# Cross attention of one layer: the queries put into the four row groups by sixteen on-chip transfers, and the order of TensorE, ScalarE and GpSimd that goes with it

## What is computed

```python
w1, w2, w3 = (w_sim[:d], w_sim[d:2 * d], w_sim[2 * d:])
Sim = (encoder_hc @ w1)[:, :, None] + (decoder_hq @ w2)[:, None, :] + jnp.einsum('bid,bjd->bij', encoder_hc * w3, decoder_hq) + b_sim[0]
A = jax.nn.softmax(Sim, axis=2)
hq_hat = jnp.einsum('bij,bjd->bid', A, decoder_hq)
Batt = jax.nn.softmax(jnp.max(Sim, axis=2), axis=1)
hc_bar = jnp.einsum('bi,bid->bd', Batt, encoder_hc)[:, None, :]
hc_hat = jnp.broadcast_to(hc_bar, encoder_hc.shape)
feats = jnp.concatenate([encoder_hc, hq_hat, encoder_hc * hq_hat, encoder_hc * hc_hat], axis=-1)
hcq = feats @ W_qv + b_qv
```

## Time and profile before

| | |
|---|---|
| median of 3 timed runs | 1349.12 us (1347.23 to 1350.66) |
| the profiled execution | 1346.48 us, of which span 1344.7 us |
| busy, PE | 1229.2 us (91%), x10417 |
| busy, DVE / POOL / ACT | 733.2 us (55%) / 708.3 us (53%) / 337.5 us (25%) |
| attention, from the span's start to the last store of x1 | about 690 us |
| the rest (recurrence, experts) | about 655 us, not touched |

### The profile page before, as it was taken

The page is one execution under the profiler, slowest core; times in us unless marked ns, Lnnn a source line. Parts: engine busy times, 40 slices in busy tenths (PEclk is TensorE's granted clock), DMA queues, the critical chain, the costliest instruction groups (busy, mean ns, idle before and its releaser), DMA issues. The chain is left out here.

```text
span 1344.7 us, 29581 instructions
## 1 busy us (share of the span) xinstructions
PE 1229.2 (91%) x10417; PEld 732.7 (54%) x10418; DVE 733.2 (55%) x1573; ACT 337.5 (25%) x768; POOL 708.3 (53%) x762
## 2 busy tenths in 40 slices
PE   0899999999999999999979799999499999999994
PEld 0444434444434444434447556666388888888883
DVE  4555666555566555567249768888722322332335
ACT  2222233222233232233135311112311111111110
POOL 1055534355544355544229766787297653540872
PEclk9999999999999999999979899999599999999997
DMA  8645554435564445554145568863214444321556
GB/s 284 227 147 205 212 211 134 155 143 200 211 211 138 151 146 197 211 211 143 70 153 163 156 214 274 293 212 111 101 48 150 146 156 149 127 83 62 149 167 185
DMA packets 99376, 225.45 MB, mean 168 GB/s; under 512 B 14152, under 2 KB 30664, under 8 KB 95216
## 3 DMA queue, kind: packets, MB, share of 16 engines
q1 hardware_dynamic: 87872, 189.46, 41.0%
q0 software_dynamic: 10288, 33.57, 7.4%
q10 hardware_dynamic: 1152, 1.57, 0.4%
HBM read 179.21 MB, written 45.35 MB: 167 GB/s over the span
## 5 line engine op out<-in xcount | busy, mean ns | idle before, releaser
L326 POOL TENSOR_TENSOR wb<-w,hcb 128x512 f32<-128x512 f32 x120 | 122.3, 1040 | 314.7 <-DVE hcb L683 292.6
L401 PE MATMUL S<-ctxT,x 32*64 32x416 f32 (+1 forms) x4096 | 185.1, 511 | 15.9 <-DVE ctxT L627 15.9
L401 PEld LDWEIGHTS S<-ctxT,x 32*64 32x64 f32 x4096 | 108.7, 133 | 94.5 <-issue 45.8
L329 POOL TENSOR_TENSOR wb<-wb,w 128x512 f32<-128x512 f32 x120 | 150.2, 1273 | 0.0
L609 DVE STREAM_TRANSPOSE ctxT<-ctx_one 128x1024 f32<-128x1024 f32 (+1 forms) x128 | 115.0, 949 | 11.7 <-DMA ctx_one<-in_ctx_dram 11.5
L436 PE MATMUL O<-ctx_one,probsT 128*64 128x512 f32 (+1 forms) x448 | 110.4, 608 | 0.0
L522 ACT ACTIVATE x<-S,w2R,w3R 128x128 f32<-128x128 f32 x256 | 92.9, 474 | 19.5 <-PE S L392 19.5
L1938 POOL TENSOR_TENSOR w_low<-w_low,w_high 128x2048 fp32r<-128x2048 f32 x21 | 96.8, 4611 | 1.7
L2123 DVE TENSOR_TENSOR f_hL<-f_TH,f_hH 128x512 fp32r<-128x512 f32 x39 | 27.0, 693 | 120.4 <-ACT f_hH L2076 117.3
L634 DVE TENSOR_REDUCE mx<-S 128x1 f32<-128x832 f32 x16 | 16.4, 1025 | 128.1 <-PE S L401 128.1
L1454 PE MATMUL Pb<-WrT,yT 128*32 128x128 f32 x2016 | 69.0, 278 | 8.3 <-DVE yT L1714 7.7
(11 more groups left out here) (286 smaller groups left out, 2504.8 us busy)
## 6 DMA issues: line engine op xcount, KB each, us to landing
ctx_one<-in_ctx_dram SPq DMA_DIRECT2D x64, 512.0 KB, 4.5
x<-in_ctx_dram SPq DMA_DIRECT2D x16, 1536.0 KB
ctx_two<-in_ctx_dram SPq DMA_DIRECT2D x16, 1536.0 KB, 9.3
ctx_one<-in_ctx_dram SPq DMA_DIRECT2D x64, 256.0 KB, 5.5
w_low<-_L_ffn_gate_up_proj_dram POOLq DMA_DIRECT2D x10, 1024.0 KB, 8.0
f_xt<-routed_x SPq DMA_DIRECT2D x39, 256.0 KB
routed_y<-f_yt SPq DMA_DIRECT2D x39, 256.0 KB
w_low<-_L_ffn_gate_up_proj_dram SPq DMA_DIRECT2D x6, 1024.0 KB, 8.6
```

The costliest lines, as they stand in the source:

```text
L326: pool.tensor_tensor(wb[:, slot, b], w3[:, c], hcb[:, c, b, None].to_broadcast([P, D]), ALU.mult).then_inc(wb_step, 1)
L329: pool.tensor_tensor(wb[:, slot, b], wb[:, slot, b], w0[:, c], ALU.add).then_inc(wb_ready, 1)
L401: last = pe.matmul(S[64 * b:64 * b + 64, a, 0:tiles * Q], qr[a * Q:(a + 1) * Q, k, 64 * b:64 * b + 64], ctxT[a * Q:(a + 1) * Q, 0:tiles, b ...
```

## The change

PE no longer spreads. `turn_early(f)` transposes the normed tokens into O (free at that time) directly behind the scores of the pair before; ACT's `queries(f)` takes it with w3c and w2c (now one column for each chunk of 128 features) into the new tile q3; and `replicate` issues sixteen transfers of 32 partitions x 512 elements from q3 into qr, on SP ahead of everything else in its step (for the first pair on ACT's queue). The scores wait for q_in, which counts them. `turn_tokens` and hcT remain for the own product.

The own product of chunk 0 stands behind the values, that of chunk 1 behind the turning of hqh, and Y's accumulation begins with it. The multiplication in the own weights goes from POOL to ACT (`scale_own`); POOL keeps the addition. brow's product goes from n=5 to n=3 of the values, and DVE's look-ahead transpose 5 goes behind hcb.

```diff
-        qr = x2[:, 2 * TWO:2 * TWO + C, :].rearrange("p c (e i) -> p (c e) i", e=QUADS)
+        qr = x2[:, 2 * TWO:2 * TWO + C, :].rearrange("p e (c i) -> p e c i", c=C)
+        q3 = sb("q3", [P, C, P])
...
+        def replicate(eng):
+            for e in range(QUADS):
+                for a in range(QUADS):
+                    eng.dma_start(qr[a * Q:(a + 1) * Q, e], q3[e * Q:(e + 1) * Q]).then_inc(q_in, 16)
...
-                for a in range(QUADS):
-                    rows = slice(a * Q, (a + 1) * Q)
-                    sp.dma_start(w2R[rows, :], w_sim[D:2 * D].rearrange("(k s) -> s k", s=Q)).then_inc(const_in, 16)
-                    sp.dma_start(w3R[rows, :], w_sim[2 * D:3 * D].rearrange("(k s) -> s k", s=Q)).then_inc(const_in, 16)
+                sp.dma_start(w2c[:], w_sim[D:2 * D].rearrange("(c p) -> p c", p=P)).then_inc(const_in, 16)
+                sp.dma_start(w3c[:], w_sim[2 * D:3 * D].rearrange("(c p) -> p c", p=P)).then_inc(const_in, 16)
...
+                sp.wait_ge(q_ready, C * (p + 2))
+                replicate(sp)
...
             def own_weights(p, c):
 
                 slot = c % 2
-                if later(p, 1) or c >= 2:
-                    pool.wait_ge(wb_used, C * p + c - 1)
-                for b in range(2):
-                    pool.tensor_tensor(wb[:, slot, b], w3[:, c], hcb[:, c, b, None].to_broadcast([P, D]), ALU.mult).then_inc(wb_step, 1)
...
-                    pool.wait_ge(hcb_done, p + 1)
...
+            def turn_early(f):
+
+                pe.wait_ge(hc_ready, f + 1)
+                for c in range(C):
+                    last = pe.transpose(O[:, c * P:(c + 1) * P], tok_rows[:, c * P:(c + 1) * P], ident[:])
+                last.then_inc(q_full, 1)
...
                 pe.wait_ge(hqh_ready, p)
+                pe.wait_ge(q_ready, C * (p + 1 if step == "last" else p + 2))
...
-                    if n == 2 and step != "last":
-                        spread_queries(p + 1, 1 - s, (0, 1))
...
-                    if n == 5:
+                    if n == 3:
...
                     values(p, s, step)
-                    if front:
-                        spread_queries(f, fs, (2, 3))
+                    pe.wait_ge(hcb_step, p + 1)
+                    own_product(p, s, (0,))
                     pe.wait_ge(hqh_ready, p + 1)
                     turn_tile(0, "hqh", tok_rows, p, step)
+                    own_product(p, s, (1,))
...
-                    product(hqT, 0, range(C), True)
-                    own_product(p, s, range(half))
+                    product(hqT, 0, range(C))
...
-                    pe.wait_ge(q_ready, DB * (f + 1))
+                    pe.wait_ge(q_in, 16 * QUADS * QUADS * (f + 1))
+                    pe.wait_ge(hcT_ready, f + 1)
                     scores().then_inc(qk_done, 1)
+                    if loads is not None:
+                        turn_early(f + 1)
...
+            def scale_own(p, c):
+
+                if later(p, 1) or c >= 2:
+                    act.wait_ge(wb_used, C * p + c - 1)
+                for b in range(2):
+                    act.activation(wb[:, c % 2, b], w3[:, c], ACT.Copy, scale=hcb[:, c, b:b + 1]).then_inc(wb_step, 1)
+
...
+                    act.activation(q3[:, c, :], O[:, c * P:(c + 1) * P], ACT.Identity,
+                                   scale=w3c[:, c:c + 1], bias=w2c[:, c:c + 1]).then_inc(q_ready, 1)
...
+                if step == "full":
+
+                    act.wait_ge(hcb_done, p + 1)
+                    if first(p):
+                        act.wait_ge(wqv_in, 32)
+                    scale_own(p, 0)
+                    scale_own(p, 1)
...
-                if front:
-                    queries(f, 2)
-                    queries(f, 3)
+                if step == "full":
+                    scale_own(p, 2)
+                    scale_own(p, 3)
                 if loads is not None:
 
                     act.wait_ge(s1_ready, f + 1)
                     norm(f + 1)
+                    queries(f + 1)
...
-                    turn_ahead(f, fs, None, (4, 5))
+                    turn_ahead(f, fs, None, (4,))
...
+                if front and back:
+                    turn_ahead(f, fs, None, (5,))
```

More of the change, by code:

```diff
@@ L123, in cross_attention @@
         bqv_b = sb("bqv_b", [P, D])
-        spread = sb("spread", [P, P])
-        w2R = sb("w2R", [P, DB])
-        w3R = sb("w3R", [P, DB])
+        w2c, w3c = sb("w2c", [P, C]), sb("w3c", [P, C])
         bsim_b = sb("bsim_b", [P, 1])
@@ L172, in cross_attention @@
         xb_ready = sem("xb_ready")
-        q_full, q_ready = sem("q_full"), sem("q_ready")
+        q_full, q_ready, q_in = sem("q_full"), sem("q_ready"), sem("q_in")
         hcT_full, hcT_ready = sem("hcT_full"), sem("hcT_ready")
@@ L245, in _ @@
             sp.dma_start(w1_b[:], bcast_row(w_sim[0:D])).then_inc(const_in, 16)
-            with nc.allow_non_contiguous_dma(reason="two small weight vectors, a column for each block of 32"):
-                for a in range(QUADS):
-                    rows = slice(a * Q, (a + 1) * Q)
-                    sp.dma_start(w2R[rows, :], w_sim[D:2 * D].rearrange("(k s) -> s k", s=Q)).then_inc(const_in, 16)
-                    sp.dma_start(w3R[rows, :], w_sim[2 * D:3 * D].rearrange("(k s) -> s k", s=Q)).then_inc(const_in, 16)
+            with nc.allow_non_contiguous_dma(reason="two small weight vectors, a column for each chunk"):
+                sp.dma_start(w2c[:], w_sim[D:2 * D].rearrange("(c p) -> p c", p=P)).then_inc(const_in, 16)
+                sp.dma_start(w3c[:], w_sim[2 * D:3 * D].rearrange("(c p) -> p c", p=P)).then_inc(const_in, 16)
             sp.dma_start(bsim_b[:], bcast_row(b_sim)).then_inc(const_in, 16)
@@ L385, in turn_tokens @@
                 last.then_inc(hcT_full, 1)
-            def spread_queries(f, fs, blocks):
-                pe.wait_ge(hcT_ready, f + 1)
-                for e in blocks:
-                    rows = slice(e * Q, (e + 1) * Q)
-                    pe.matmul(S[:, e, :], spread[rows, :], hcT[fs][rows].rearrange("p c i -> p (c i)"),
-                              start=True, stop=True).then_inc(q_full, 1)
+            def turn_early(f):
[3 more added lines that the diff above has]
+                last.then_inc(q_full, 1)
             def scores():
@@ L400, in scores, with product @@
                         for b in range(2):
-                            last = pe.matmul(S[64 * b:64 * b + 64, a, 0:tiles * Q], qr[a * Q:(a + 1) * Q, k, 64 * b:64 * b + 64],
+                            last = pe.matmul(S[64 * b:64 * b + 64, a, 0:tiles * Q], qr[a * Q:(a + 1) * Q, k % QUADS, k // QUADS, 64 * b:64 * b + 64],
                                              ctxT[a * Q:(a + 1) * Q, 0:tiles, b, k, :], start=(k == 0), stop=(k == DB - 1))
                 return last
-            def product(lhsT, w, chunks, start):
+            def product(lhsT, w, chunks):
                 for c in chunks:
-                    last = pe.matmul(Y[:], lhsT[:, c, :], w12[:, w + c, :], start=start and c == 0, stop=(w > 0 and c == C - 1))
+                    last = pe.matmul(Y[:], lhsT[:, c, :], w12[:, w + c, :], start=False, stop=(w > 0 and c == C - 1))
                 return last
@@ L479, in body @@
                 if back:
-                    product(f3, C, range(half, C), False).then_inc(y_done, 1)
+                    product(f3, C, range(half, C)).then_inc(y_done, 1)
                 if front:
@@ L515, in tokens, with queries @@
                 act.copy(hcT[fs][:], S[:, QUADS - 1, :].rearrange("p (c i) -> p c i", c=C)).then_inc(hcT_ready, 1)
-            def queries(f, e):
-                act.wait_ge(q_full, QUADS * f + e + 1)
+            def queries(f):
+                act.wait_ge(q_full, f + 1)
+                if later(f, 1):
+                    act.wait_ge(q_in, 16 * QUADS * QUADS * f)
                 for c in range(C):
-                    k = c * QUADS + e
-                    act.activation(qr[:, k, :], S[:, e, c * P:(c + 1) * P], ACT.Identity,
-                                   scale=w3R[:, k:k + 1], bias=w2R[:, k:k + 1]).then_inc(q_ready, 1)
+                    act.activation(q3[:, c, :], O[:, c * P:(c + 1) * P], ACT.Identity,
+                                   scale=w3c[:, c:c + 1], bias=w2c[:, c:c + 1]).then_inc(q_ready, 1)
             def body(p, s, step, loads):
@@ L532, in body @@
                 else:
+                    queries(f)
+                    act.wait_ge(q_ready, C)
+                    replicate(act)
                     tokens(f, 0)
-                if front:
-                    if later(f, 1):
-                        act.wait_ge(qk_done, f)
-                    queries(f, 0)
-                    queries(f, 1)
+                if step == "full":
[4 more added lines that the diff above has]
+                    scale_own(p, 1)
                 if back:
@@ L577, in body @@
                     tokens(f + 1, s if back else 1)
-            for e in range(QUADS):
-                rows = slice(e * Q, (e + 1) * Q)
```

(4 more changed lines are left out.)

14 lines of the change are left out of this document (5 added, 9 removed).

## The result

The changed kernel takes 1357.25 us (median of 9 runs, 1353.79 to 1363.30), the kernel before 1348.71 (9 runs): a ratio of 1.0056, 95% interval [1.0041, 1.0072]. Forecast was 1309, a gain of 3%. The profiled execution has a span of 1356.0 us against 1344.7. The attention ends (first matmul of the stage behind it) at 699.4 in place of 690.1, +9.3; what follows is 2.0 longer. So nearly all of the loss lies in the stage that the change was to shorten. The two traced executions differ by 11.3 us, the medians by 8.5: the traced execution of the kernel before is 2.2 us faster than its median.

What follows compares the result with a forecast made beforehand. TensorE's own order of work was taken as the bound: 14 periods x 2.36 = 33.0, plus 2.9, 1.7 and 2.5, gave 40.1 us off the profiled 1346.48, so 1306.4; with 2.6 for the median, 1309 us, range 1304 to 1327.

Steps and rivals of the forecast that it cites:

- the cost of one transfer on SP's queue: Behind the scores: sixteen 64 KB issues on SP at 0.45 us each, 6.9 to 8.6 us in all, nothing late.
- Rival 3: Slower: transfers of t us each hold SP's queue, waiting 16t - 8.2 per period; gain gone at t = 0.66; chance 0.07.
- the margin of the part loads: Before the scores: the parts' last transposes end 0.4 to 1.5 us before PE needs them; queue lateness 0 to 0.8.
- rival 1: Each period: slipping margins (brow, exponentials, part loads) lose 0.3 to 1.3 us; 1314 to 1329, middle 1320; chance 0.23.
- PE's own sum: PE's work per attention period: 2.89 us off, 0.53 on, so 2.36 saved, 40.24 to 37.88.
- E to V: Stretch from the scores' end (E) to the values' start (V): 7.50 us before, 8.03 in the new order.
- spread and turn_early: Spread inside the values goes, -1.06 us; four transposes behind the scores come, +0.53.
- own product: Two chunks fill PE's pauses between the values and product(hqT), in place of standing behind it: -1.83 us per period.
- The small margins: Inside a period: brow hidden by 0.2 us, ACT's queries before the exponentials by 0.3, own weights ready in time.
- Rival 2: Own weights come late, hcb not moving forward; with all 1.83 lost, 0.53 per period remains: 1336; chance 0.05.
- x_sb: Next pair's input arrives 10.5 us after ctx_two's issue, at V+23.1; norm done V+26.2, before scores end at V+29.9.
- The start: Before the first scores: fewer small weight issues ahead of the loads; bounds 2.9 off and 1.4 on, 2.5 us off taken.

Runs made afterwards that it cites:

- earlier first release: Against the kernel with POOL issuing the transfers: context parts of 1, 2, 2, 1 tiles, released behind values steps 0, 2, 4, 6; 1320.62 us.
- with POOL: Against the changed kernel: POOL instead of SP issues all sixteen transfers, behind a one-column product; 1320.55 us, ratio 0.9791.
- the fastest one: Against the kernel with POOL issuing the transfers: SP loads x_sb first and issues ctx_two only when the last part has landed; 1314.5 us, ratio 0.9748.
- the five larger ones: Against the changed kernel: on SP, q3 goes once to device memory and back in four reads, 256 KB each, replacing sixteen transfers; 1323.66 us, ratio 0.9817.

## Why the prediction was wrong, step by step

- **The step that failed: the cost of one transfer on SP's queue.** I took 0.45 us, between 0.43 (two ctx_two issues in 0.85) and 0.54 (24 stores in 12.98). It was 0.627, outside both bounds. The 0.43 came from loads out of device memory, the 0.54 from stores into it; on-chip copies were not in the trace, and I let the bounds stand as if they were. Rival 3 had the mechanism and nearly the size: at t = 0.627 its 16t - 8.2 gives 1.8 us of waiting per period against 2.5 measured. Its break-even of 0.66 lay 0.03 from what came. A chance of 0.07 for a case whose deciding value stood 0.12 from a bound taken from another kind of transfer was too small. The 0.7 between 1.8 and 2.5 is in good part the step from the sixteenth issue to the first part load, 0.93 in the period shown (265.92 to 266.85), where the sum had 0.4 for the store. By rival 3's sum 0.627 alone would still have left a gain of 0.53 per period, about 1337; the loss came with the longer waits and the slower scores below.
- **The second failed step: the margin of the part loads.** "Parts 1 to 3 are released about 1 us earlier" was true and worth nothing (earlier first release: 10.3 us of pauses against 9.6). What I took as 0.4 to 1.5 was under 0.4: without any transfer there were still 5.7 us of pauses. The forecast set the landing by the release; with the release in time it hangs on what else is on the transfer engines (the order of the loads alone, with POOL as issuer, took 6.0 of the 9.6 us of pauses away). That ctx_two moves forward with the shorter values was nowhere in it. This is rival 1's case, and it held for the kernels without the first fault: 1320.55 with POOL, beside its middle of 1320. That the two agree so closely is luck in part: 4.8 us of the 1320.55 lie behind the attention, where the rival had nothing.
- **Not in the prediction at all: the slowed scores.** 13.9 us, of which 12.4 at the lower granted clock, brought on by the pause; 0.9 in the third pair, 0.2 in the last and 0.3 in the first at 1.00, from a cause that no run tells. The sum took every pause at its length. With 37.7 us of pauses alone the changed kernel would have been about equal to the one before.
- **PE's own sum held.** Product(hqT) starts at 276.24 - 273.78 = 2.46 behind the values, to the digit; values 12.30 for 12.44; E to V 7.89 for 8.03; busy 37.70 for 37.88. Where the loads are light or well ordered and PE has no pause, the period is 37.55 to 37.67. Inside it two terms were off in opposite ways: spread and turn_early 1.0 for 0.53, own product 1.57 for 1.83.
- **The small margins held.** brow's product waits for nothing, by 0.21 us (it starts at 265.42, brow is written by 265.21); the four queries on ACT end at 255.87 = E+2.28 (forecast 2.2), and the exponential waits for nmx by 0.26, so they are hidden; hcb is done at V+6.3 (6.4), ACT's multiplications take 2.56 for four, 0.64 each and 0.71 alone (0.69), and the own product never waits for POOL. Rival 2 is out.
- **x_sb** came at V+26.2, not V+23.1, 13.8 us behind ctx_two's issue in place of 10.5; why longer was not tried. It cost nothing, since the scores end at V+32.5.
- **The start**: scores at 33.65 for 35.41, 1.8 gained where 2.5 was taken. ACT's sixteen issues held it 10.27 us, and what PE waited for last there is the copies (x<-q), 0.4 behind DVE's last transpose (33.29).

What stays open: the stages behind the attention are 2.0 us longer in the changed kernel, 4.8 with POOL and 4.1 in the fastest one, though nothing in them is changed. With POOL and in the fastest it lies in the recurrence (167.0 and 167.4 us against 162.1 before); in the changed kernel 0.9 of the 2.0 does (163.0). In the kernel with POOL some 6 us in the middle of the recurrence are at a lower clock behind a thin stretch, which the kernel before and the changed one do not show, as in these two windows of the kernel with POOL (here the columns are PE busy, clock, DMA share, GB/s):

```profile
770.40:774.40 4.00, 1.33 (x33) 0.96 0.77 271
774.40:778.40 4.00, 4.00 (x38) 0.50 0.18 61
```

Whether the shorter attention shifts the loads behind it, or something else does, no run here tells.

## What to carry to other kernels

Issues are a resource of the queue's engine, counted by the piece: before putting n of them ahead of a load that PE waits for, multiply n by a duration of the same kind of transfer, and where the trace has none of that kind, give values past the bounds a real chance: here 0.627 in place of 0.45 took 1.8 of the 2.36 us that each period was to gain, before anything else went wrong. Put them on an engine that is idle just then, and give the load that is wanted first the transfer engines for itself. And price a pause of PE above its length: here 37.7 us of pauses brought 12.4 us of slower products with them.

## What the runs showed of the hardware

- An on-chip transfer takes 0.59 us (median of 240, 0.51 to 0.71) of SP, 0.627 from one to the next, alike for 64 KB and 32 KB; the same on POOL takes 7.88 / 16 = 0.49, on ACT 10.27 / 16 = 0.64. A part load from device memory takes SP 0.34 (median of 128). The transfers land 2.0 us after their issue at the median (1.9 to 7.5), while a new one goes out every 0.627, so they overlap, as the forecast read it.
- Sixteen issues held SP for 10.03 us, the five larger ones for 3.8, and 34 us of the kernel's time lie between the two; moving the sixteen to POOL brought 37. The Trainium skill (DMA: Bandwidth & Descriptors, Rules for kernel authors) wants small transfers coalesced, above all under 64 KB, which is just the size of these; that was right here, by way of the issuer's time. The Trainium skill, same page (Issuing engines are not separate DMA queues), says that issuing from several engines saves only the sequencer's time, "which is usually small relative to the DMA itself". The first half agrees with these runs; the second doesn't hold where the issues stand in a row: 0.627 us each against 2.0 to land, and the issue time was the loss.
- A pause in an otherwise full PE was followed by a granted clock of 0.80 to 0.88 over the scores behind it (13 to 14 us) in 7 of 15 cases, with pauses of 1.90 to 3.39 us. In the other eight, with pauses of 1.38 to 3.07, the clock stayed at 1.00. Length alone does not tell the two apart: 3.07 before the window at 242.24 left it at 1.00, 1.90 before the scores at 322.18 brought 0.87. In the earlier trace rows it was 1.00 throughout.
